# Edge weighting in a graph aggregation, moved from VectorE to ScalarE, with one-hots compared tile by tile

## The reference

```
deg = maximum(segment_sum(ones, dst, 6250), 1)
xn  = layernorm(x)
agg = segment_sum(edge_weight[:, None] * xn[src], dst, 6250)
```

## Time and profile before

| what | value |
|---|---|
| time, median of 3 runs | 3971.13 us (3969.26 to 3977.46) |
| profiled execution, its own time | 3973.01 us |
| its span, first to last instruction | 3971.2 us |
| mean granted TensorE clock | 0.881 of full |
| first aggregation | about 164 to 1209 us |
| second aggregation | about 1773 to 2780 us |
| third aggregation | about 2780 to 3790 us |

### The profile page before, as it was taken

How to read it: one execution, slowest core, us unless ns; L and a number is a source line. 1 busy time by engine, 2 the same in 40 slices (tenths; PEclk the granted TensorE clock), 3 DMA queues, 4 the chain that set the end, 5 groups by cost and what they waited for, 6 DMA issues and landing times. The chain is left out here.

```text
span 3971.2 us, 42640 instructions
## 1 busy us (share of the span) xinstructions
PE 2855.2 (72%) x13014; PEld 2164.6 (55%) x13014; DVE 1763.2 (44%) x4542; ACT 781.5 (20%) x1777; POOL 2553.1 (64%) x2689
## 2 busy tenths in 40 slices
PE   6767767777767747787777766665577777777878
PEld 5555555555554435575555545444455565666647
DVE  6544444444443752353333333222355555555533
ACT  2211111111112313331111101001122222222220
POOL 3477777777770252447777777776777777777701
PEclk9888888888888879898999988887899999999869
DMA  3343444444433356774444433333444444444405
GB/s 110 95 121 115 120 120 115 120 121 119 117 116 88 119 161 204 222 220 118 125 125 125 119 111 112 111 111 95 119 127 130 130 128 126 130 130 130 127 27 195
DMA packets 281073, 501.73 MB, mean 126 GB/s; under 512 B 61307, under 2 KB 181505, under 8 KB 280698
## 3 DMA queue, kind: packets, MB, share of 16 engines
q0 software_dynamic: 126240, 345.85, 30.2%
q1 hardware_dynamic: 137452, 139.10, 11.3%
q10 hardware_dynamic: 17136, 13.84, 1.1%
HBM read 412.72 MB, written 85.58 MB: 125 GB/s over the span
## 5 line engine op out<-in xcount | busy, mean ns | idle before, releaser
L1308 PE MATMUL bank<-g,m 128*128 128x256 f32 (+1 forms) x4704 | 1542.8, 454 | 882.6 <-DMA g<-d_t,src_i 555.3
L1231 POOL DMA_INDIRECT g<-d_t,src_i x1568 | 1508.2, 962 | 513.9 <-issue 513.9
L1308 PEld LDWEIGHTS bank<-g,m 128*128 128x128 f32 x4704 | 915.1, 221 | 1198.8 <-issue 401.7
L1231 POOL DMA_INDIRECT g<-d_xn,src_i x784 | 795.3, 1014 | 254.9 <-issue 254.9
L1256 DVE TENSOR_SCALAR m<-iota,rel_f,ew_f 128x128 f32<-128x128 f32 x1568 | 420.6, 361 | 326.8 <-PE bank L1308 321.3
L1272 DVE TENSOR_TENSOR accT<-bank,accT 128x256 f32 x294 | 122.7, 417 | 666.9 <-PE bank L1296 666.6
L1237 ACT ACTIVATE s<-bank 128x256 f32<-128x256 f32 (+1 forms) x294 | 111.6, 380 | 921.5 <-PE bank L1308 464.8
L1259 DVE TENSOR_TENSOR eq<-iota,rel_f 128x1024 bf16<-128x1024 f32 x98 | 119.9, 1223 | 48.2 <-PE bank L1310 47.8
L1310 PE MATMUL bank<-ones_b,eq 128*128 128x1 bf16 x784 | 139.3, 178 | 0.0
L219 POOL TENSOR_TENSOR rsd<-ved,mhalf 128x2 f32<-128x2 f32 (+1 forms) x25 | 18.9, 757 | 180.7 <-DVE ved L213 180.5
L1172 PE MATMUL bank<-wg,side_lg 128*128 128x256 f32 (+1 forms) x392 | 130.1, 423 | 2.9 <-DVE side_lg L1164 2.9
(11 more groups left out here) (388 smaller groups left out, 4285.5 us busy)
## 6 DMA issues: line engine op xcount, KB each, us to landing
g<-d_t,src_i POOLq DMA_INDIRECT x1568, 2.7
g<-d_xn,src_i POOLq DMA_INDIRECT x784, 2.8
side_xn<-d_xn SPq DMA_DIRECT2D x96, 128.0 KB, 2.5
d_x<-x SPq DMA_DIRECT2D x48, 256.0 KB, 3.7
d_swT<-wkv SPq DMA_DIRECT2D x48, 256.0 KB, 3.5
swT<-d_swT SPq DMA_DIRECT2D x24, 512.0 KB, 3.3
xt<-d_xs POOLq DMA_DIRECT2D x80, 128.0 KB, 2.8
d_ys<-y ACTq DMA_DIRECT2D x80, 128.0 KB, 2.4
```

The costliest lines, as they stand in the source:

```text
L1231: pool.indirect_dma_start(g[n % RING][:, u, 0:D], None, table, bass.IndirectOffsetOnAxis(ap=k.src_i[:, t:t + 1], axis=0)).then_inc(gathere ...
L1308: ins = pe.matmul(b[:, 0:GW], m[o][:, u, :], g[r][:, u, :], start=(u == 0), stop=(u == GT - 1 and not count))
```

## The change

In the first aggregation only, `prepare` no longer makes `m`. It makes `eq` in eight instructions of one tile each, every one a comparison of `iota` with one scalar pointer, the tile's column of `rel_f`. A new function `weigh` on ScalarE makes `m` from `eq`, in eight ACTIVATEs of one tile each, a copy with the tile's column of `ew_f` as scale. It waits for `eq_done` of its group and, as `prepare` does, for TensorE to be done with the buffer of three groups before. Groups 0 and 1 are weighted ahead of the rounds, and then group 2i + 2 at slot 1 and group 2i + 3 at slot 9, each behind the window copy of that slot.

```
         def main_act(act):
...
+            def weigh(n):
+
+                if n >= NG or not count:
+                    return
+                r = n % ONEHOTS
+                wait(act, eq_done, n + 1)
+                wait(act, multiplied, n - ONEHOTS + 1)
+                for u in range(GT):
+                    t = n * GT + u
+                    ins = act.activation(m[r][:, u, :], eq[r][:, u, :], ACT.Copy, scale=k.ew_f[:, t:t + 1])
+                ins.then_inc(m_done, 1)
+            weigh(0)
+            weigh(1)
             for i in range(ROUNDS):
                 for slot in range(2 * GT):
                     if slot == 1 and 0 < i <= NB:
                         copy(2 * i - 1)
+                    if slot == 1:
+                        weigh(2 * i + 2)
                     if slot == 9 and i < NB:
                         copy(2 * i)
+                    if slot == 9:
+                        weigh(2 * i + 3)
                     at_step(side.act, slot, i)
...
-                dve.tensor_tensor(eq[r][:], k.iota[:].rearrange("p (a n) -> p a n", a=1).to_broadcast([P, GT, P]),
-                                  k.rel_f[:, e].rearrange("p (u a) -> p u a", a=1).to_broadcast([P, GT, P]), ALU.is_equal).then_inc(eq_done, 1)
-                wait(dve, eq_done, n + 1)
-                dve.tensor_tensor(m[r][:], eq[r][:], k.ew_f[:, e].rearrange("p (u a) -> p u a", a=1).to_broadcast([P, GT, P]), ALU.mult).then_inc(m_done, 1)
+                for u in range(GT):
+                    t = n * GT + u
+                    ins = dve.tensor_scalar(eq[r][:, u, :], k.iota[:], k.rel_f[:, t:t + 1], None, ALU.is_equal)
+                ins.then_inc(eq_done, 1)
```

## The result

| | before | after |
|---|---|---|
| median | 3971.89 us (4 runs) | 3935.25 us (4 runs, 3931.8 to 3938.56) |
| ratio | | 0.9906, 95% interval 0.9889 to 0.9923 |
| profiled execution, span | 3971.2 us | 3937.1 us |

The account below looks back on a forecast made before the run. GpSimd's back-to-back gathers were taken to bound the first aggregation: 48.4 us off the gathers, 1.5 back for the side chain, so -47 from 3973.0 to 3926, and 3924 us as median (1.9 lower); range 3914 to 3945.

Parts of the forecast that it names:

- GpSimd's train of gathers sets the stage: First aggregation: GpSimd issues 784 gathers back to back, TensorE waits for them; faster gathers save 48.4 us.
- rival (d): First aggregation: TensorE takes over the pace when gathers get faster, half the gain lost, 3948 us; chance 0.05.
- A gather is held at its start by an instruction with two SBUF inputs, not by a busy VectorE: First aggregation: early in a gather GpSimd needs something eq holds, then takes 0.82 us; excess 51 us a stage.
- One input in SBUF does no harm: New comparisons, judged by L1256 in the second aggregation: gathers beside them undisturbed, excess there 3 us.
- rival (b): First aggregation: each new comparison holds a gather to its own end, 35 us (3957) or 18 us (3940); chance 0.12.
- Rival (c): First aggregation: gathers held to the comparison train's end, 103 us against 51, 4023 us, or 4091 if stopped throughout; chance 0.05.
- The side chain: First aggregation, L685, L702, L736, two SBUF inputs each: may meet gathers once timing shifts, 0 to 9 us, 1.5 taken.
- The rest of the program stays: Outside the first aggregation: later aggregations as now, 2 or 3 us either way from the clock's phases.
- TensorE's wait for gathers: First aggregation: TensorE's waiting for gathered rows was to be about 255 us in place of 304.
- ScalarE and its queue cost nothing: First aggregation: weighting takes 2.5 us a group, and the delayed copy L616 still serves TensorE in time; cost zero.
- The length of a train of eight comparisons: First aggregation, VectorE: eight one-pointer TENSOR_SCALARs a group take 1.7 to 2.1 us, below the removed 2.45.
- The rule of the Trainium skill: VectorE beside gathers: two-port tensor_scalar locks GpSimd out throughout, tensor_tensor not seen stalling DMAs; 120 us slower, 4091.

Follow-up runs that it names:

- eq_psum: Kernel before with weighting on ScalarE and eq still one broadcast instruction, its index row iota copied to PSUM: 3931.97 us, ratio 0.9900.
- weigh_only: Kernel before with only the weighting moved to ScalarE, eq still one broadcast instruction over 1024 elements: 3970.72 us, ratio 0.9994.
- eq_only: Kernel before with only the comparisons made tile by tile, m still one VectorE instruction over 1024 elements: 3977.6 us, ratio 1.0019.
- tt_tiles: The change, but each tile's comparison a TENSOR_TENSOR with rel_f broadcast, so two SBUF inputs: 3933.06 us, ratio 0.9900.
- side_psum: The change, with one input of each of L685, L702 and L736 kept in PSUM: 3920.64 us, ratio 0.9872.
- weigh_twice: The change with every ScalarE weighting done twice, a wait between: 3928.59 us, ratio 0.9888.

## Why the prediction was right, and where its size was off

- **GpSimd's train of gathers sets the stage.** Right where it was made: 42.1 us off the gathers, 42.1 us off first to last start, in the profile. On the two slower chips GpSimd waits for TensorE, as in rival (d), and the change wins nothing.
- **A gather is held at its start by an instruction with two SBUF inputs, not by a busy VectorE.** Right for eq, and shown: eq_psum takes one input away and the hold is gone, weigh_only takes half the work away and next to nothing is won. What I held of m was too mild: "isn't disturbed by m" is true of a gather that is past its start, and eq_only shows m holding gathers as eq does.
- **One input in SBUF does no harm.** Wrong. The step was the reading of L1256 beside gathers from a single gather of 0.94 us. The TENSOR_SCALARs with one input hold gathers as well, to their own end. That is the first half of rival (b), at another price: 5.7 us, not 18 or 35, since a gather waits at most some 0.12 us and mostly once. The forecast charged 3 us, what the second aggregation shows, so it lost little by this. It also means that most of the gain is to be had by shorter instructions alone, as tt_tiles shows: two inputs kept, and 36.4 of 42.0 us won. Rival (c), 103 us and more, is out for trains of eight, but the long train of tt_tiles did hold one gather to its end.
- **The side chain.** This is the term that was mis-sized. Its three instructions were given 1.5 us out of 0 to 9; the gathers beside them have 6.4 us of excess, and side_psum takes that to nothing. The three cost less before because eq had set the gathers' rhythm: with eq holding (weigh_only) the excess beside L702 and L736 is 2.2 us, with eq in PSUM (eq_psum) 6.9.
- Together: the forecast put the gathers at 746.9 + 1.5 = 748.4 us, and they came to 753.3, which is 4.9 more. The side chain adds 4.9 to it and the comparisons 2.7, and the plain gather, 0.946 us as median in place of 0.949, takes 2.4 off; the remaining 0.3 lies in the other gathers.
- **The rest of the program stays.** The stage's train of gathers is 42.1 us shorter and the span 34.1: 8 us elsewhere. Over the ten profiles on chips at 3971 us, the time between the first aggregation's last side step and the second's first gather is 563.0 to 572.1 us, at a mean granted clock of 0.86 to 0.89, longest where the clock was lowest (572.1 at 0.86, 563.0 at 0.89). So a part of it goes with the clock of that run. Whether a shorter first aggregation also makes for a lower clock after it is not settled.
- **TensorE's wait for gathers** was to fall from 304 to 255 us. It fell to 271.2, 33 in place of 49; no run separates why.
- **ScalarE and its queue cost nothing.** Right: 2.44 us a group against 2.5, TensorE not waiting for L616, and weigh_twice shows the margin.
- **The length of a train of eight comparisons.** 1.66 us against 1.7 to 2.1.
- **The rule of the Trainium skill**, "SBUF — State Buffer", "Who interferes with whom". I quoted that a tensor_scalar in a two-port mode locks GpSimd out for its whole length. No trace names the mode that the comparisons run in. The ends of the gathers agree with the rule (57 of 58 in the change end 0.81 to 0.83 us behind the end of a comparison), with two bounds: a gather that is past its start isn't held, and at 0.28 us a comparison it comes to 5.7 us in all. The same section says that an instruction with two SBUF inputs contends with a GpSimd instruction that reads SBUF. I set it aside for its neighbour on DMA descriptors; weigh_only against eq_psum agrees with it, 39.1 us of gather time for one input, and so does eq_only.

## What to carry to other kernels

Where GpSimd's indirect DMAs set the pace, look in the timeline for those that are longer than the median and for what VectorE had begun before them: every VectorE instruction with two SBUF inputs is a candidate, and so is a TENSOR_SCALAR that reads SBUF. As an estimate the cost goes with the square of the instruction's length; the runs agree in direction (eight comparisons of 0.28 us in place of one of 1.22) but don't measure the power. Cut it into short ones, or put one of two inputs in PSUM; moving work to another engine is needed for neither. Take away all such instructions together, since the longest hides the others by setting the rhythm, and check on a chip with a lower clock whether the pace is still set there.

## What the runs showed of the hardware that I had not expected

- A gather begun in a train of 23 TENSOR_TENSORs of 0.28 us lasted 3.85 us, to 0.84 us behind the train's end; in trains of eight none lasted over 1.32 us.
- VectorE's one-input comparisons in trains cost the gathers 3.6 (side_psum) and 5.7 us (the change) a stage, one broadcast comparison with its other input in PSUM 0.04 us (eq_psum).
- Two of the chips ran the same kernel 12% slower, 4446 and 4452 us against 3972, at a mean granted clock of 0.80 and 0.81 against 0.88, with stretches about once a round in which matrix products are recorded 0.69 us apart.
